# A four-layer graph attention kernel: the receivers' rows of the attention weights fetched on all partitions by DMA instead of made there by TensorE transposes

## The reference

```python
Wh = h @ W
s_i, s_j = Wh @ a1, Wh @ a2
e = leaky_relu(s_i[:, :, None] + s_j[:, None, :])     # one number per pair of nodes
e = where(adj, e, -inf)
out = softmax(e, axis=-1) @ Wh                        # then elu or relu, added to x
```

## Time and profile before

| | us |
|---|---|
| median of 3 runs | 3268.5 (3265.84 to 3269.47) |
| the profiled execution | 3268.22 |
| its span, first to last instruction | 3266.4 |
| TensorE matmuls busy | 3148.4 |
| VectorE busy | 2689.4 |
| ScalarE busy | 1864.1 |
| GpSimd busy | 326.2 |

### The profile page before, as it was taken

One profiled execution on the slowest core, in us unless ns is written; L12 is line 12 of the kernel. 1 busy time (PEld: TensorE's weight loads), 2 busy tenths in 40 slices (PEclk: granted clock), 3 DMA queues, 4 the chain that ended last, 5 costly groups with the idle time before them and its releaser, 6 DMA issues.

```text
span 3266.4 us, 55502 instructions
## 1 busy us (share of the span) xinstructions
PE 3148.4 (96%) x20480; PEld 2860.2 (88%) x20480; DVE 2689.4 (82%) x7611; ACT 1864.1 (57%) x4627; POOL 326.2 (10%) x265
## 2 busy tenths in 40 slices
PE   5899999999999999999999999999999999999996
PEld 4888899889889888889988889988989988989985
DVE  5578888888888888888888888888888888888865
ACT  1355556565655565655565655655655655655653
POOL 0011100111100111110111110111110111110010
PEclk7799999999999999999999999999999999999997
DMA  2000000000000000000000000000000000000000
GB/s 65 14 1 14 14 14 1 14 14 14 14 14 1 14 14 14 14 14 1 14 14 14 14 14 3 12 14 14 14 14 8 7 14 14 14 14 7 1 7 13
DMA packets 16332, 41.32 MB, mean 13 GB/s; under 512 B 5312, under 2 KB 6848, under 8 KB 16064
## 3 DMA queue, kind: packets, MB, share of 16 engines
q1 hardware_dynamic: 16064, 37.77, 3.3%
HBM read 20.99 MB, written 16.78 MB: 12 GB/s over the span
## 4 chain that ended last, share of the span: by engine, by line
PE 88%; POOL 4%; ACT 4%; DVE 2%; issue 1%; DMA 1%; SPq 0%; POOLq 0%; ACTq 0%; DVEq 0%
PE bank L399 30%; PE bank L457 20%; PE bank L526 14%; PE bank L489 14%; POOL oTlo L1031 4%; PE bank L445 3%; PE bank L413 3%; PE bank L538 2%; ACT O L915 1%; ACT oThi L917 1%; PE bank L435 1%; PE bank L563 1%; ACT Z L978 0%; PE bank L345 0%; DVE x L846 0%
## 5 line engine op out<-in xcount | busy, mean ns | idle before, releaser
L457 PE MATMUL bank<-hw,R 128*128 128x257 f32 x3072 | 735.9, 383 | 6.2 <-ACT Z L983 3.2
L457 PEld LDWEIGHTS bank<-hw,R 128*128 128x128 f32 x3072 | 566.9, 190 | 108.1 <-issue 24.6
L489 PEld LDWEIGHTS bank<-hw,R 128*128 128x128 f32 x4096 | 515.5, 196 | 17.1 <-issue 7.4
L489 PE MATMUL bank<-hw,R 128*128 128x65 f32 x4096 | 515.0, 274 | 7.3 <-DVE R L653 7.3
L526 PE MATMUL bank<-hw,R 128*128 128x257 f32 (+1 forms) x2048 | 492.9, 380 | 0.0
L653 DVE SCALAR_TENSOR_TENSOR R<-bank,E,mask_ne 128x512 f32<-128x512 f32 x640 | 452.6, 742 | 1.4 <-PE bank L445 1.2
L1024 POOL TENSOR_TENSOR rs<-ve,mhalf 128x4 f32<-128x4 f32 x128 | 145.8, 1139 | 2683.0 <-DVE ve L600 2683.0
L526 PEld LDWEIGHTS bank<-hw,R 128*128 128x128 f32 x2048 | 372.6, 189 | 46.1
L399 PE MATMUL bank<-wfc_hi,oThi 128*128 128x256 f32 (+1 forms) x1024 | 303.3, 296 | 30.6 <-POOL oTlo L1031 29.4
L874 ACT COPY Z<-bank 128x258 f32<-128x258 f32 (+1 forms) x640 | 239.0, 374 | 161.6 <-PE bank L399 157.4
L399 PE MATMUL bank<-wfc_lo,oThi 128*128 128x256 f32 (+1 forms) x1024 | 289.4, 283 | 0.0
(11 more groups left out here) (199 smaller groups left out, 6828.4 us busy)
## 6 DMA issues: line engine op xcount, KB each, us to landing
x<-in_x_dram SPq DMA_DIRECT2D x32, 512.0 KB, 3.2
out_dram<-x SPq DMA_DIRECT2D x32, 512.0 KB, 2.6
R<-in_adj_dram SPq DMA_DIRECT2D x2, 512.0 KB, 4.5
R<-in_L_gnn_mlp_w_dram SPq DMA_DIRECT2D x2, 512.0 KB, 3.9
R<-in_L_gnn_W_fc_dram SPq DMA_DIRECT2D x2, 512.0 KB, 4.2
R<-in_L_gnn_W_dram SPq DMA_DIRECT2D x3, 256.0 KB, 4.0
R<-in_L_gnn_W_hand_dram SPq DMA_DIRECT2D x1, 256.0 KB, 2.6
Z<-in_L_gnn_a_dram SPq DMA_DIRECT2D x8, 0.2 KB, 3.5
```

Of the source, the lines that this page charges most:

```text
L457: ins = e.matmul(bk[:, 0:257], P[:, j, i * 128:(i + 1) * 128], hw[:, j, 0:257], start=(j == 0), stop=(j == NBLK - 1))
L489: ins = e.matmul(bk[:, i * 66:i * 66 + 65], P[:, (4 * h + j) % PTILES, i * 128:(i + 1) * 128], hv[:, j, h, 0:65], start=(j == 0 and i == 0 ...
```

## The change

The eight `row` steps leave TensorE and their eight uses leave the banks' rings; the copy to `rowt` leaves ScalarE. SP's steps are now made by a generator on SP too, `sync_batch`, in an order of its own. In step l, once `E[:, 0]` is there, SP writes it to a DRAM scratch `rowd` (4 bytes per piece: 2048 pieces for the four heads of step 0, 512 for each other step), waits until this has landed, and reads the 2 KB row back to all 128 partitions (256 KB per row). Rows 0, 3, 4, 5, 6 and 7 go into `rowt`, one after the other; rows 1 and 2 go in one DMA into columns of `hw` that are free in step 0. `weigh` waits for the DMA and reads its row from SBUF, with the same arithmetic. So there are 12 more DMAs per batch: 5 writes and 7 reads. The orders of all engines are new.

```diff
@@ SHARED, ONCE
-    "h": (5, 4), "raw": (5, 4), "sc": (5, 5), "TM": (5,), "E": (5, 3), "row": (8,),
+    "h": (5, 4), "raw": (5, 4), "sc": (5, 5), "TM": (5,), "E": (5, 3),
+    "P": (8, 4), "rowd": (5,), "rowl": (6,), "rowm": (1,), ...
@@ TURNS
+    "pe": (
+        "1ww11200www2w22wwwwww22ww120111ww100101w2w2ww1w0222212w1111w1w111www1ww1w112222ww222w100100221w00202"
+        "20221102010101111020w00211211w2112121200"),
+    "dve": (
+        "www1w1wwwww00wwwww0ww022ww22202ww022w22w22ww22wwwww22222w22w1ww1ww222w2wwww0ww2w2w01w2w1w1ww210wwwww"
+        "0ww100010111201222012011w2222222211110122220100222012221102110200212111110w1100200201011200202000002"
+        "w21000122202w2"),
+    "act": (
+        "1111020222221220221122ww11001012w211112202211212121121121121w222w11111w22011221222121222121212011011"
+        "2111212112101"),
+    "pool": (
+        "111w122w2w0"),
+    "sp": (
+        "11020202021121"),
@@ build
+        def row_tile(s, p):
+            if p in (1, 2):
+                return hws[s][:, 2 * p - 2:2 * p, 264:520]
+            return rowt[s][:, :].rearrange("p (a n) -> p a n", a=2)
@@ tensor_batch
-            def row(p, l, h):
-                w.wait_ge(*freed(b, "row", p))
-                w.wait_ge(*at("E", b, l, 0))
-                bk = bank_of(b, "row", p)
-                for n in range(NBLK):
-                    i = e.transpose(bk[:, n * 128:(n + 1) * 128], m["E"][:, 0, h, n:n + 1].broadcast_to([128, 128]),
-                                    ident[:, :])
-                i.then_inc(up("row", b))
-                yield
@@ weigh
-                w.wait_ge(*at("row", b, p))
+                if p in (1, 2):
+                    w.wait_ge(*landed(b, "rowm", 0))
+                else:
+                    w.wait_ge(*landed(b, "rowl", 0 if p == 0 else p - 2))
-                    e.scalar_tensor_tensor(P[:, t, :], bank_of(b, "row", p)[:, :], m["E"][:, 1, h, j:j + 1],
-                                           mask[:, j, :], ALU.max, ALU.mult).then_inc(up("P", b))
+                    e.scalar_tensor_tensor(P[:, t, :].rearrange("p (a n) -> p a n", a=2), row_tile(s, p),
+                                           m["E"][:, 1, h, j:j + 1], mask[:, j, :].rearrange("p (a n) -> p a n", a=2),
+                                           ALU.max, ALU.mult).then_inc(up("P", b))
@@ scalar_batch
-            w.wait_ge(*at("row", b, 4))
-            e.copy(rowt[s][:, 0:512], bank_of(b, "row", 4)[:, :]).then_inc(up("rowc", b))
-            yield
@@ sync_batch
+            def spread(p, l):
+                w.wait_ge(*landed(b, "rowd", l))
+                if p == 3:
+                    w.wait_ge(*at("P", b, 0, 3))
+                to = rowd[s, p if l == 0 else 0, :].rearrange("(a n) -> a n", a=2)
+                e.dma_start(row_tile(s, p), to.partition_broadcast(128)).then_inc(up("rowl", b), 16)
+                yield
+
+            def write(l, nh):
+                w.wait_ge(*at("E", b, l, 0))
+                if l:
+                    w.wait_ge(*landed(b, "rowl", l))
+                elif b >= LANES:
+                    w.wait_ge(*landed(b - LANES, "rowl", 5))
+                e.dma_start(rowd[s, 0:nh, :].rearrange("h (n p) -> p h n", p=128), m["E"][:, 0, 0:nh, :],
+                            allow_slow_non_contiguous=True).then_inc(up("rowd", b), 16)
+                yield
+
+            yield from write(0, 4)
+            yield from spread(0, 0)
+            to = rowd[s, 1:3, :].rearrange("h (a n) -> (h a) n", a=2)
+            e.dma_start(hws[s][:, :, 264:520], to.partition_broadcast(128)).then_inc(up("rowm", b), 16)
+            yield
+            yield from spread(3, 0)
+            yield from write(1, 1)
+            yield from spread(4, 1)
+            yield from write(2, 1)
+            yield from spread(5, 2)
...
+            yield
+            yield from write(3, 1)
+            yield from spread(6, 3)
+            yield from write(4, 1)
+            yield from spread(7, 4)
...
@@ block.sync
+            in_turns(lambda b: sync_batch(e, w, b), TURNS["sp"], lambda: iter(()))
```

More of the change, by code:

```diff
@@ L43 @@
     [("hT0", k, "hTlo", (0, k)) for k in range(2)] + [("h0", i, "raw", (0, i)) for i in range(4)]
-    + [("TM0", 0, "sc", (0, 1)), ("row", 0, "P", (0, 3))]
-    + [u for h in range(4) for u in (
-        ([("row", h + 1, "P", (h + 1, 3))] if h < 3 else []) + [("att0", h, "y0", (h,))])]
+    + [("TM0", 0, "sc", (0, 1))]
+    + [("att0", h, "y0", (h,)) for h in range(4)]
     + [("hT1", k, "hTlo", (1, k)) for k in range(2)] + [("m1", i, "m1a", (i,)) for i in range(4)]
     + [("h1", i, "raw", (1, i)) for i in range(4)]
-    + [("TM1", 0, "sc", (1, 1)), ("hs2", 0, "hw2", (0,)), ("row", 4, "rowc", (0,))]
-    + [("hs2", i, "hw2", (i,)) for i in range(1, 4)]
+    + [("TM1", 0, "sc", (1, 1))] + [("hs2", i, "hw2", (i,)) for i in range(4)]
     + [("attf", q, "ef", (q, 1)) for q in range(8)] + [("zT", k, "o2", (k,)) for k in range(4)]
@@ L53 @@
     + [("r3", i, "r3c", (i,)) for i in range(2)]
[L54 removed]
+    + [("h2", i, "raw", (2, i)) for i in range(4)] + [("TM2", 0, "sc", (2, 1))]
     + [("att0b", i, "yh", (i,)) for i in range(4)]
     + [("hT2", k, "hTlo", (2, k)) for k in range(2)] + [("h3", i, "raw", (3, i)) for i in range(4)]
[L57 removed]
+    + [("TM3", 0, "sc", (3, 1))] + [("att1b", i, "e2", (i, 1)) for i in range(4)]
     + [("hT3", k, "hTlo", (3, k)) for k in range(2)] + [("S", 1, "Sb", (1,))]
     + [("h4", i, "raw", (4, i)) for i in range(4)]
[L60 removed]
+    + [("TM4", 0, "sc", (4, 1))] + [("att2b", i, "y3", (i,)) for i in range(4)]
 )
@@ L153, in build @@
         hT = [{p: sb(f"hT{s}{p}", [128, 2, N], F32R) for p in PARTS2} for s in range(LANES)]
-        hws = [sb(f"hw{s}", [128, NBLK, 514]) for s in range(LANES)]
+        hws = [sb(f"hw{s}", [128, NBLK, 520]) for s in range(LANES)]
         hvs = [hws[s][:, :, 0:264].rearrange("p b (h n) -> p b h n", n=66) for s in range(LANES)]
+        rowd = nc.dram_tensor("rowd", [LANES, NBLK, N], F32)
         rowt = [sb(f"rowt{s}", [128, N]) for s in range(LANES)]
@@ L478, in tensor_batch @@
             yield from top(0, 4)
-            yield from row(0, 0, 0)
             for h in range(4):
-                if h < 3:
-                    yield from row(h + 1, 0, h + 1)
                 w.wait_ge(*freed(b, "att0", h))
@@ L510, in tensor_batch @@
             for n in range(NBLK):
-                if n == 1:
-                    yield from row(4, 1, 0)
                 w.wait_ge(*freed(b, "hs2", n))
@@ L569, in tensor_batch @@
             yield from top(2, 1)
-            yield from row(5, 2, 0)
             yield from attend(0, 2, 5)
@@ L577, in tensor_batch @@
             yield from top(3, 1)
-            yield from row(6, 3, 0)
             yield from attend(1, 3, 6)
@@ L586, in tensor_batch @@
             yield from top(4, 1)
-            yield from row(7, 4, 0)
             yield from attend(2, 4, 7)
@@ L719, in vector_batch @@
             w.wait_ge(*at("E", b, 1, 1))
[L720 removed]
+            w.wait_ge(*landed(b, "rowl", 2))
             for j in range(NBLK):
```

32 lines of the change are left out of this document (15 added, 17 removed), and 4 rows, old and new, of tables (ONCE, SHARED).

## The result

Median 4463.3 us (4460.5 to 4470.2, 4 runs) against 3268.8 before on the same chip: ratio 1.366, interval [1.364, 1.368]. The prediction was 3248, range 3180 to 3320. It was wrong: slower had 0.30, and its price stood at 3341.

What follows compares the result with a forecast made beforehand. It took TensorE, almost without holes, as the bound: 93.1 work + 2.6 hole + 0.7 other holes = 96.4 us per period against 97.5. Over 29 periods 32 us saved, less 12 at the ends, gave 3248 us, range 3180 to 3320.

Steps and rivals of the forecast that it cites:

- The write of 512 pieces of 4 bytes: Write of a single row to DRAM on SP's queue: lands in 2.2 us, bounds 2.0 and 3.5.
- the four-fold: Step 0's write of 2048 pieces: 4.0 us, between 2.2 and 8.8, the latter four times the whole of 2.2.
- the slower rival: First `weigh` of step 0: each microsecond of `write0` over 4.8 delays rDf2 and `attf`; at 8.0, 3341 us; chance 0.30.
- The read of 256 KB: Reading a row back to all partitions: 2.6 us, in series after the write, 5.2 together with semaphores.
- Row 5's landing: End of the period: lands 6.2 us after `top` of step 2, not late because four `hn` lie between.
- Work on TensorE: Per period 96.5 - 3.4 = 93.1 us, with eight rows removed at 0.42 us each.
- The hole before `m1.0`: End of the period: TensorE stands 2.6 us waiting for VectorE's `hTlo1`, from the order and not a DMA.
- ScalarE's list: ScalarE's serial steps from `A` of step 2 to `hThi1`, ending 5.3 us after `top` of step 2.
- The ends: Start and end of the run, with fewer batches to hide behind: 12 us lost in all.
- booked at nothing, bounds 0 and 3: Step 2's weights, now with two SBUF inputs, beside GpSimd's subtractions: 0, up to 3 us of VectorE's time per period.
- the copy on ScalarE: The copy to `rowt` leaves ScalarE, which is no bound (58 of 97.5 us), so no value.
- VectorE no bound: VectorE 83.05 us busy per period, 14 us behind TensorE before the change and only 10 after it.

Runs made afterwards that it cites:

- apart_then_input: Changed kernel, reads fetching input rows after each write's landing, written 4-byte pieces 512 bytes apart in DRAM: 3254.9 us, 0.996 of the kernel before.
- no_rows: Changed kernel with its new orders but no row written or fetched, weights computed from a constant SBUF tile: 3202.3 us, 0.979 of the kernel before.
- flip: Changed kernel plus a small VectorE transpose per step, so writes take 128 pieces of 128 bytes: 3299.3 us, 1.009 of the kernel before.
- close_then_input: Changed kernel, writes unchanged (pieces 4 bytes apart), reads fetching input rows after each write's landing: 4553.5 us, 1.393 of the kernel before.
- the meter: Kernel before with nine DMAs added per batch on SP's queue, each waited for before the next: 3282.4 us, 1.004 of the kernel before.

## Why the prediction was wrong, step by step

**Failed: the landing of the writes, and of the reads behind them.** "The write of 512 pieces of 4 bytes: the nearest row is a load of as many pieces, 2.2 us" with 3.5 as the upper bound, and 4.0 for 2048 with 8.8 above. Measured 7.9 to 9.5 and 11.9; both lie outside my bounds, so the range could not hold the time. The nearest row was a load: it reads scattered pieces and writes into SBUF, and the runs show that such pieces are cheap in that direction and dear when they are put side by side in DRAM. Its second use, for the four-fold, made 8.8 the worst case, but from 128 pieces on the count is hardly a factor. By the slower rival's own rule the measured 11.9 would give 3268.5 + 29 x (7.1 - 1.1) + 12 = 3455, so `write0` alone is not the 1192 us either.

**Failed with it: the read, "The read of 256 KB: 2.6".** Reads issued with no write on their way took 4.6 to 5.3 in the change, `spread3` 8.0 and `spread0` 11.5 (medians); these two went out behind a close write that had not landed. My sum had write and read of one row in series, but nowhere a read held up by the write of another row. Where the writes land early the read is a small term: 3.2 to 4.2 us in apart_then_input, whose whole time is 3255.

**Right in kind, far off in size: the slower rival.** Its place (the first `weigh` of step 0, then rDf2 and `attf`) and its sign (a releaser DMA into `rowt`) are the trace's. It took one write as late, and its reads at 3.2 at most. All five writes were late: step 1's row, which I had not examined, made VectorE stand 9.1 us, row 5 8.0 ("Row 5's landing is not late there"), row 0 14.0, and `write3` queued behind `write0` lands 14 us after its issue.

**The period, by its terms.** From no_rows' 93.85 to 133.77 are 39.9 us. TensorE's holes grew by 27.8 (2.1 to 29.9), and the same 604 matmuls took 12.1 more (91.78 to 103.88) as the granted clock fell from 1.00 to 0.85. The second term had no place in my sum at all: holes of 6 to 12 us came with a lower clock and did not only cost themselves. With 29 periods at 35.8 more than before (means 132.87 and 97.07) come 1038 of the 1192 us of span; the rest lies at the start and the end, where I had 12.

**Mis-sized: order, work and ends.** Work on TensorE is 91.8 instead of 93.1: I took a row at 0.42 us from start to start, 3.4 for eight, and the group of the kernel before had 4.7 per batch (149.8 us over 32 batches):

```profile
L445 PE MATMUL bank<-identr,E 128*128 128x128 f32 x1024 | 149.8, 274 | 4.7 <-ACT E L882 4.7
```

The hole before `m1.0` is 1.6 instead of 2.6 (ScalarE's list adds up to 5.15 by its own terms, where I wrote 5.3; that is the smaller part of it), and the periods at a granted clock of 0.98 are dearer by 1.5; together 94.2 instead of 96.4 as the mean. The ends, booked at 12, cost 16 us in no_rows and 36 in apart_then_input (time up to the second store and after the 31st, against the kernel before). So it is in part luck that apart_then_input, where the writes land in about 2 us as I had assumed, comes to 3254.9 and so close to my 3248: a smaller hole and less work are paid back by the ends, the reads and the clock.

**GpSimd, "booked at nothing, bounds 0 and 3".** Nothing in the change itself (748 ns, since its rows come so late); 2.1 us per period in flip. A row that comes one or two microseconds late is enough.

**Held:** weights at 747 ns against 742, the copy on ScalarE at no value, VectorE no bound (79.8 of 133.8).

## What to carry to other kernels

Price a DMA write by its own kind: where no row shows small pieces written side by side to DRAM, the bound above is not four times a load, and one run with that DMA alone in the queue settles it. Look also at what is issued behind it: a read of 3 to 5 us took 8 to 12 there. Before a layout goes through DRAM, turn it on chip so that the pieces are long: 128-byte pieces after a 0.2 us transpose landed in 1.4 to 1.9 us, where 4-byte ones took 9.5; a stride put on a reader instead left both kernels 12 and 24% behind the kernel before. And when long waits are added, count the work between them at the lower clock as well: here 12.1 of the 39.9 us per period.

## What the runs showed of the hardware that was not expected

- A read issued on the same queue while close 4-byte pieces are on their way to DRAM landed only after them, in each of the 27 middle periods of the changed kernel and of close_then_input, whatever it read: medians of 8.0 to 11.5 us in the changed kernel and 9.3 to 10.3 for reads of the input, 3.7 to 4.2 with the pieces 512 bytes apart.
- The first read of a row after its small-piece write is slower than the same read again, 5.5 against 3.3; after a write in one 2 KB piece it took 3.1 to 3.4. Whether that is the row or the time after the write is not shown.
- The weights with two SBUF inputs are as quick on VectorE as with one in PSUM (746 against 742 ns) until GpSimd subtracts beside them (1266 ns on the mean of flip's 128 of step 2).

The landing itself. In the meter's trace the 512 close pieces, issued at 1859.00, had all been moved 1.5 us later; the landing came at 9.5 us. The DMA engines are idle meanwhile, DMA share 0.00:

```profile
1860.50:1868.40 7.90, 7.04 (x38) 5.68 (x36) 7.70 (x16) 6.03 (x11) 5.58 (x4) 1.00 0.00 0
```

The Trainium skill, DMA: Bandwidth & Descriptors, Anatomy of one DMA, says of DMAs issued from GpSimd that most of their fixed time, some 2 us, is the wait for the receipt of the last write by the target memory. The trace of this DMA, issued from SP, agrees with the place and not with the size: 8 us from the last piece moved to the landing.
